# A third transposed tile per state read out by ScalarE and added by GpSimd, in a decoder layer with a selective scan

## The reference

```python
def _selective_scan(u, dt, A, Bm, Cm, D):
    def step(h, xs):
        u_t, dt_t, b_t, c_t = xs
        dA = jnp.exp(dt_t[:, :, None] * A[None])
        h = dA * h + (dt_t * u_t)[:, :, None] * b_t[:, None, :]
        y = jnp.einsum('bds,bs->bd', h, c_t) + D * u_t
        return (h, y)
...
p1 = jnp.einsum('bsh,eoh->bseo', nf, mlp1_weight) + mlp1_bias
g = jnp.minimum(p1[..., 0::2], LIMIT)
lin = jnp.clip(p1[..., 1::2], -LIMIT, LIMIT)
act = g * jax.nn.sigmoid(ALPHA * g) * (lin + 1.0)
p2 = jnp.einsum('bsei,ehi->bseh', act, mlp2_weight) + mlp2_bias
combined = jnp.einsum('bseh,bse->bsh', p2, combine)
```

## Time and profile before

| | us |
|---|---|
| median of 3 runs (lowest, highest) | 1700.97 (1700.62, 1701.95) |
| the profiled execution | 1699.97 |
| its span in the trace | 1698.2 |

### The profile page before, as it was taken

How to read it: one execution, slowest core, us unless ns; L and a number is a source line. 1 busy time by engine, 2 the same in 40 slices (tenths; PEclk the granted TensorE clock), 3 DMA queues, 4 the chain that set the end, 5 groups by cost and what they waited for, 6 DMA issues and landing times.

```text
span 1698.2 us, 23130 instructions
## 1 busy us (share of the span) xinstructions
PE 1314.0 (77%) x5582; PEld 857.7 (51%) x5582; DVE 1405.5 (83%) x1829; ACT 934.7 (55%) x1369; POOL 970.2 (57%) x529
## 2 busy tenths in 40 slices
PE   6965545699877777799867777799867787798698
PEld 4434334466345555566345554566344455466375
DVE  6159999887789999888689999978689999962597
ACT  3264443323777767523777767623777767711464
POOL 1059888630588888620588888621488978620000
PEclk9986666699899989999989889999989979996699
DMA  6111111011111112020111112020211121010111
GB/s 219 54 35 38 37 49 38 28 35 34 63 38 56 56 51 68 7 75 33 52 51 56 47 58 69 7 76 20 65 50 54 39 66 53 25 50 1 63 53 59
DMA packets 53348, 86.13 MB, mean 51 GB/s; under 512 B 8245, under 2 KB 33986, under 8 KB 53259
## 3 DMA queue, kind: packets, MB, share of 16 engines
q1 hardware_dynamic: 49993, 82.89, 15.0%
q10 hardware_dynamic: 3266, 2.21, 0.4%
HBM read 74.51 MB, written 10.57 MB: 50 GB/s over the span
## 4 chain that ended last, share of the span: by engine, by line
PE 38%; DVE 28%; issue 14%; ACT 13%; POOL 4%; DMA 2%; DVEq 1%; ACTq 1%; SPq 0%; POOLq 0%
DVE work L1255 13%; PE ps L1462 12%; PE ps L1656 7%; DVE xt L1255 7%; DVE stage L1293 6%; ACT ps L891 6%; PE ps L1678 4%; PE ps L1628 2%; PE ps L1457 2%; POOL work L642 2%; PE ps L1560 2%; ACT work L922 2%; ACT ps L917 2%; PE ps L1562 2%; PE ps L1470 2%
## 5 line engine op out<-in xcount | busy, mean ns | idle before, releaser
L1656 PE MATMUL ps<-ident,work 128*128 128x128 f32 x1536 | 313.0, 329 | 287.0 <-DVE stage L1293 184.7
L1255 DVE TENSOR_TENSOR_SCAN work<-ps,work 128x1024 f32<-128x1024 f32 x192 | 438.4, 2284 | 19.6 <-ACT ps L891 12.1
L1656 PEld LDWEIGHTS ps<-ident,work 128*128 128x128 f32 x1536 | 191.9, 161 | 418.9 <-DVE stage L1293 246.2
L891 ACT ACTIVATE ps<-dt,a_neg 128x1024 f32<-128x1024 f32 x256 | 284.9, 1117 | 190.9 <-DVE work L1255 149.8
L642 POOL TENSOR_TENSOR work<-dtu,b_bc 128x1024 f32<-128x1024 f32 x128 | 299.9, 2372 | 56.9 <-PE ps L1656 53.1
L1293 DVE SCALAR_TENSOR_TENSOR stage<-ps,c_tok,stage 128x512 f32<-128x512 f32 x384 | 272.4, 734 | 25.6 <-PE ps L1656 23.4
L1678 PE MATMUL ps<-w,work 128*128 (+1 forms) x1024 | 274.8, 418 | 1.8 <-DVE work L1400 1.8
L1678 PEld LDWEIGHTS ps<-w,work 128*128 128x128 f32 x1024 | 219.5, 217 | 52.9 <-issue 9.5
L1628 PE MATMUL ps<-nfT,w 128*128 128x512 bf16 x512 | 169.3, 430 | 32.0 <-DVE work L1330 17.9
L642 POOL TENSOR_TENSOR work<-dtu,w_out 128x1024 f32<-128x1024 f32 x64 | 149.3, 2353 | 44.1 <-PE ps L1656 44.1
L658 POOL TENSOR_TENSOR stage<-stage,work 128x512 f32<-128x512 f32 x128 | 160.2, 1275 | 15.9 <-ACT work L907 15.9
(11 more groups left out here) (142 smaller groups left out, 1937.6 us busy)
## 6 DMA issues: line engine op xcount, KB each, us to landing
b_bc<-b_rows SPq DMA_DIRECT2D x32, 512.0 KB, 3.7
w_out<-b_rows SPq DMA_DIRECT2D x32, 512.0 KB, 4.0
wbc<-combine_rows SPq DMA_DIRECT2D x64, 256.0 KB, 3.4
stage<-in_x SPq DMA_DIRECT2D x8, 512.0 KB, 4.2
xt<-in_x SPq DMA_DIRECT2D x8, 512.0 KB, 5.4
x_rows<-xt SPq DMA_DIRECT2D x4, 1024.0 KB, 4.7
res<-x_rows SPq DMA_DIRECT2D x8, 512.0 KB, 4.1
out_x<-res SPq DMA_DIRECT2D x8, 512.0 KB, 3.3
```

The lines of the kernel that those rows point to most:

```text
L891: act.activation(decay_in(d, alone, opening), dt[:, d, :], ACT.Exp, scale=a_neg[:, bass.ds(it * 2 + (d * N + hf * (N // 2) + par), 1)]).th ...
L1255: dve.tensor_tensor_scan(h, decays, h, 0.0, ALU.mult, ALU.add).then_inc(scan_done, 1)
L1656: mm = pe.transpose(ps[:, a % HT_BANKS, d * P:(d + 1) * P], slot(par, d)[:, a * P:(a + 1) * P], ident[:, :])
```

## The change

Tile 7 (`LATE`) joins tiles 0 and 1 (`EARLY`) in being read out by ScalarE and added by GpSimd; there are three such tiles in a state and still two buffers, used in rotation. VectorE sums tiles 2 to 6. On each engine:
- ACT: evict of tile 7 stands after tanh 1 and add 1, ahead of linear_in 1.
- POOL: the add of tile 7 of a state stands one turn later, after product 0 of that turn; at the end of a row it stands behind the others.
- DVE: sums 2, 3; (scan 1) gate product 0, sum 4; (scan 2) sum 5, linear product 0; (scan 3) sum 6, gate product 1.
- PE: up(1,0) goes ahead of the transposes of tiles 6 and 7; down j=0 follows these. The waits for banks 0 and 1 follow the new readers: tile 1 waits for the evict of tile 7 of the state before, tile 7 for sum 5.

```diff
@@ -189,8 +189,10 @@
         GATE_BANK, LINEAR_BANK = 4, 5
-        EVICTED = 2
+        EARLY, LATE = (0, 1), (TT - 1,)
+        EVICTED = len(EARLY) + len(LATE)
         SUMMED = TT - EVICTED
+        EVICT_BUFFERS = 2
@@ -402,7 +404,8 @@
         ITS = N // 4
-        DBU_CREDIT, SCAN_CREDIT, HT_CREDIT, HT_READY_CREDIT = 8, 4, HT_BANKS, 16
+        DBU_CREDIT, SCAN_CREDIT, HT_CREDIT, HT_READY_CREDIT = 8, 4, 1, 16
+        EVICT_CREDIT = 1
         EX_CREDIT = 2
@@ -573,7 +576,7 @@
             pool.sem_inc(aw_ready, EX_CREDIT)
-            pool.sem_inc(evict_added, EVICTED)
+            pool.sem_inc(evict_added, EVICT_BUFFERS)
             for i, value in enumerate((-LIMIT, ALPHA / 2 * LIMIT, 2 * LIMIT)):
@@ -651,11 +654,12 @@
-                def add_evicted(hf, it, par):
-
-                    for e in range(EVICTED):
-                        pool.wait_ge(evict_ready, (state(b, hf, it, par) - 1) * EVICTED + e + 1)
-                        pool.tensor_tensor(stage[:, e, :], stage[:, e, :], evicted[:, e, :],
+                def add_evicted(hf, it, par, back, tiles):
+
+                    for a in tiles:
+                        e = (EARLY + LATE).index(a)
+                        pool.wait_ge(evict_ready, (state(b, hf, it, par) - back) * EVICTED + (e + 1 + EVICT_CREDIT))
+                        pool.tensor_tensor(stage[:, a, :], stage[:, a, :], evicted[:, (par + back + e) % 2, :],
                                            ALU.add).then_inc(evict_added, 1)
@@ -665,9 +669,12 @@
                     pool.wait_ge(b_loaded[par], (b * 2 * ITS + hf * ITS + it) * 16 + 16)
+                    second = hf == 0 and isinstance(it, int) and it == 0
                     for d in range(CT):
                         state_product(w, par, d)
-                    add_evicted(hf, it, par)
+                        if d == 0 and not second:
+                            add_evicted(hf, it, par, 2, LATE)
+                    add_evicted(hf, it, par, 1, EARLY)
                     if bp is not None:
@@ -676,9 +683,10 @@
                 turns(pool, body)
+                add_evicted(1, ITS, 0, 2, LATE)
                 if bp is not None:
                     weigh(1, ITS, 0)
-                add_evicted(1, ITS, 0)
+                add_evicted(1, ITS, 0, 1, EARLY + LATE)
@@ -687,6 +695,7 @@
             act.sem_inc(l_ready, 1)
+            act.sem_inc(evict_ready, EVICT_CREDIT)
             for dst, name in ((qwT, "qWT"), (cwT, "cWT"), (kwT, "kWT"), (vwT, "vWT"), (owT, "oWT")):
@@ -897,15 +906,16 @@
                     act.wait_ge(dve_scaled, 5)
-                def evict(hf, it, par):
+                def evict(hf, it, par, tiles):
...
                     n = it * 2 + (hf * (N // 2) + par - 1)
-                    wait_apart(act, evict_added, w * EVICTED + EVICTED)
-                    for e in range(EVICTED):
-                        wait_apart(act, hT_ready, w * TT + (e + 1 + HT_READY_CREDIT))
-                        act.activation(evicted[:, e, :], ps[:, e % HT_BANKS, :], ACT.Copy,
-                                       scale=c_tok[:, e, bass.ds(n, 1)]).then_inc(evict_ready, 1)
+                    for a in tiles:
+                        e = (EARLY + LATE).index(a)
+                        wait_apart(act, evict_added, w * EVICTED + (e + 1))
+                        wait_apart(act, hT_ready, w * TT + (a + 1 + HT_READY_CREDIT))
+                        act.activation(evicted[:, (par + 1 + e) % 2, :], ps[:, a % HT_BANKS, :], ACT.Copy,
+                                       scale=c_tok[:, a, bass.ds(n, 1)]).then_inc(evict_ready, 1)
@@ -957,7 +967,7 @@
                         decay(b, bp is None, hf, it, par, 0)
-                    evict(hf, it, par)
+                    evict(hf, it, par, EARLY)
                     if bp is not None:
@@ -972,6 +982,8 @@
                         chains[1][1]()
+                    evict(hf, it, par, LATE)
+                    if bp is not None:
                         linear_in(hf, it, par, 1)
@@ -1002,9 +1014,10 @@
                 turns(act, body)
-                evict(1, ITS, 0)
+                evict(1, ITS, 0, EARLY)
                 if bp is not None:
                     clip(state(bp, 1, ITS, 0) * 2)
+                evict(1, ITS, 0, LATE)
@@ -1354,20 +1367,20 @@
                     scan(w, par, 1, decay_in(1, bp is None))
-                    accumulate(hf, it, par, 4)
-                    accumulate(hf, it, par, 5)
                     if bp is not None:
                         gate_product(s, 0)
+                    accumulate(hf, it, par, 4)
+                    if bp is not None:
                         if second:
...
                     scan(w, par, 2, decay_in(2, bp is None))
-                    accumulate(hf, it, par, 6)
+                    accumulate(hf, it, par, 5)
                     if bp is not None:
...
                     scan(w, par, 3, decay_in(3, bp is None))
-                    accumulate(hf, it, par, 7)
+                    accumulate(hf, it, par, 6)
                     if bp is not None:
@@ -1409,7 +1422,7 @@
                         linear_product(state(bp, 1, ITS, 0) - 1, 1, 1)
-                    for a in range(EVICTED, TT):
+                    for a in range(len(EARLY), TT - len(LATE)):
                         accumulate(1, ITS, 0, a)
@@ -1484,14 +1497,17 @@
-                    pe.wait_ge(hT_used, r * (N * SUMMED) + (N * SUMMED - HT_BANKS + d + 1 + HT_CREDIT))
+                    if d == 0:
+                        pe.wait_ge(hT_used, r * (N * SUMMED) + (N * SUMMED + HT_CREDIT))
+                    else:
+                        pe.wait_ge(evict_ready, r * (N * EVICTED) + (N * EVICTED + EVICT_CREDIT))
                 product(ph.bank(job), [(w_in[:, k, DI + d * P:DI + (d + 1) * P], xnT[:, k, c * HALF:(c + 1) * HALF])
...
-                    pe.wait_ge(evict_added, r * (N * EVICTED) + (N * EVICTED + EVICTED))
+                    pe.wait_ge(evict_added, r * (N * EVICTED) + (N * EVICTED + EVICT_BUFFERS))
                 if job == ("Y", 2, 0):
@@ -1648,10 +1664,12 @@
-                        if EVICTED <= a < 2 * EVICTED:
-                            pe.wait_ge(evict_ready, w * EVICTED + (a - EVICTED + 1))
+                        if a == 0:
+                            pe.wait_ge(hT_used, w * SUMMED + HT_CREDIT)
+                        elif a <= 1 + len(EARLY):
+                            pe.wait_ge(evict_ready, w * EVICTED + (a - 1 + EVICT_CREDIT))
                         else:
-                            pe.wait_ge(hT_used, w * SUMMED + (a + 1 if a < EVICTED else a - EVICTED + 1))
+                            pe.wait_ge(hT_used, w * SUMMED + (a - 1 - len(EARLY) + HT_CREDIT))
                         for d in range(CT):
@@ -1724,11 +1742,11 @@
                         up(hf, it, par, 0, 1)
+                        up(hf, it, par, 1, 0)
                     else:
...
                     if bp is not None:
-                        up(hf, it, par, 1, 0)
                         if hf == 1 and isinstance(it, int) and par == 1:
```

## The result

| | before | after |
|---|---|---|
| median of 4 runs each, us | 1701.46 | 1785.70 |
| lowest and highest | 1700.62, 1702.99 | 1783.95, 1789.98 |
| the profiled execution | 1699.97 | 1789.98 |
| its span | 1698.2 | 1788.2 |

The ratio is 1.0498, with a 95% interval of 1.0476 to 1.0520: the changed kernel is 5% slower, by 84.2 us between the medians. The forecast was 1794 in a range of 1702 to 1832.

What follows compares the result with a forecast made beforehand. VectorE, nearly full in joint turns of 15.66 us, and the decays bounded the kernel. Against the profiled 1699.97, +86 joint turns and row tails, +7 finalize, +7 openings, -6 loop alone gave +94, so 1794, range 1702 to 1832.

Steps and rivals of the forecast that it cites:

- VectorE and the decays: Joint turn: by these alone it falls from 15.66 to 15.30 us, so at most 0.36 is gained.
- The chain: Joint turn: from sum 5 over tile 7, down 0, up(1,1), linear_in 1 to decay 0; turn 15.69 full clock, 18.4 low.
- the share of low clock: Joint turn: low clock for four fifths of the chain, so 2.2 us more, a turn of 17.8.
- The clock: TensorE before tile 7: 1.25 us busy in 5.9 brings the clock down; rival that it stays up, 1704 us, chance 0.10.
- The three finalize turns: Joint turns with finalize: tile 7 moves behind one scan, 2.4 us each, 7 in all.
- The turns that open a joint loop: First turn with transposes in each joint row: same chain, 2.5 us each, 7 in all.
- The row ends: Tail of each joint row: counted as one more joint turn, 2.2 us each.
- The loop alone: Loop without joint phases: turns fall from 13.57 to about 13.1 us, -6 in all, between 0 and -9.
- this ring: Loop alone: scan 3, transposes, evict, transposes; VectorE waits 0.60 us for tile 2; claimed not to be shortened.
- GpSimd and ScalarE: Joint turn: GpSimd's added 1.25 us makes 15.4, under 15.66; ScalarE's added evict of 0.68 costs nothing by itself.
- ordinary turns: Joint turns: 36, or 39 with the row tails, each 2.2 us longer; 86 us for the 39.
- the cases: Whole time: forecast 0.76, clock stays up 0.10, faster 0.08 plus 0.02 for a mistake, slower still 0.06.

Runs made afterwards that it cites:

- the filled kernel: The changed kernel with up(0,1) computed and tile 6 transposed four times over in joint turns; 1708.39 us, ratio 1.0049.
- the filled kernel with linear_in 1 moved: The filled kernel with linear_in 1 of a turn run behind decay 0 of the next; 1708.68 us, ratio 1.0039.
- the filled run with tile 7 early: The changed kernel with sums 4 and 5 ahead of scan 2, PE reordered, up(0,1) computed four times over in joint turns; 1704.79 us, ratio 1.0022.

## Why the prediction was right

**VectorE and the decays.** The step from 15.66 to 15.30 by these alone fits the gaps that were measured: in the changed kernel the four scans start 4.11, 3.72 and 3.74 apart (542.32, 546.43, 550.15, 553.89), and it is the last gap that grew, to 5.59. No run reached 15.30 in every turn, since others ended later; the nearest were the short turns of 15.35 in the filled kernel with linear_in 1 moved.

**The chain.** The start of tile 7 was put at 10.82 after scan 0 and came at 10.82. The full-clock end was put at 15.69 and measured at 15.67 in the filled kernel. With the clock as granted I said 17.8, and the turns are 16.9 to 17.7, with 18.4 behind the finalize turn. The mean of the 36 is 17.3, 1.6 over before instead of 2.2. The term was mis-sized in the share of low clock: I took four fifths of the chain, 2.2 of 2.7. In the turn shown, 17.16 long, 1.5 of the 2.7 came. Tile 7 took the whole of its low-clock price (0.91 to down 0); down 0 took 2.73, between 1.73 and the 3.57; up(1,1) and what follows ran at the full clock.

**The clock.** The forecast rested on the earlier trace rows: a stretch in which PE had little work, without any idle time over some 2.2, and then the low clock. In the changed kernel the two idle times are 2.17 and 1.84 (I had put them at 2.1 and 2.5), hardly longer than the 2.15 of the earlier trace rows. Yet the clock fell in every ordinary turn: the granted clock of each in the first joint row is 0.80 or 0.81, where before it was 0.89 in eight turns of the twelve and 1.00 in four. The filled kernel settles it: same chain, same waits, PE busier by its repeats, and 77 of the 84 us are gone. The repeats also shorten the idle times, from 2.17 to 0.88 and from 1.84 to 1.17, so the run shows that PE's thin stretch brings the clock down, not whether its work or its gaps do. By the Trainium skill, "TensorE: Matmul & The Clock Gate", "What's actually happening", activity releases the throttle; the filled kernel agrees, with PEclk from 0.78 to 0.96. The reading of its section "HAM oscillation — how this bites in real kernels" by single long idle gaps does not hold here, where the clock falls with no gap over 2.17 in an ordinary turn, and the measurement decides.

**The other turns.** The three finalize turns cost 4.3 each (25.1 against 20.8), not 2.4; the late add had a share of 1.7 in this by its own run, which I had counted at nothing there. The turns that open a joint loop cost 7.9 in all, I had said 7 (2.5 x 3 is 7.5). The row ends cost 9.9, I had said 2.2 each.

**The loop alone.** I said -6 and it was -0.7. The step that failed is the start of the next scan 0 at 13.0 to 13.1 behind product 0: turns are 13.3 to 13.7. Two terms failed. From the end of sum 5 to product 0 I took 0.9 for tile 7, and it is about 1.3, with a granted clock of 0.50 in that stretch. And tile 0 now waits for sum 6, which stands behind scan 3, where it had waited for a sum ahead of it: the change moved the last reader of bank 0 behind the last scan. From scan 3 to sum 2 it is now 6.29 (285.69 to 291.98) where it was 5.71 (176.62 to 182.33), which takes back nearly all of the 0.65 that VectorE lost. I had said only that this ring was not shortened; that part of it was made longer. The run with sum 6 small shows that neither of the two sets the turn alone.

**GpSimd and ScalarE.** Right in ordinary turns: they have room in a turn of 17, as the run with the small add shows. Where tile 7 was early again they did not: GpSimd waits for its evict in the run with sum 5 put back, and ScalarE holds the turn of 15.64 in the filled run with tile 7 early. The prediction had no term for the late add's own wait for its evict.

**The sum.** Forecast +94 against the profiled execution, measured +90.0: ordinary turns 79 against 57.6 (58.6 in the 36, less 1.0 by which the last turns, up to the end of scan 3, got shorter), row ends 7 against 9.9, finalize 7 against 12.9, openings 7 against 7.9, loop alone -6 against -0.7, and 2.4 at the start and behind the loop alone that no term had. Between the medians it is +84.2. The total is nearer than its terms deserve, which is luck: 21 too much in the ordinary turns stand against 10 too little in the row ends, finalize turns and openings, 5 in the loop alone and 2 elsewhere. Two small slips in the working changed nothing: the chances of the cases add up to 1.02, and by them slower would be 0.87, not 0.84; and 1745 belongs to a turn of 16.6, not 16.8, once the other terms are added.

## What to carry to other kernels

When an instruction moves, ask who stands in fixed order behind the one that it releases: taking 0.65 us of VectorE's work out of each turn cost 1.6, because one sum stood behind one scan more and the chain behind it met the low clock. Where a trace shows the clock low behind stretches with little work on PE, a chain that moves there is to be priced at the low clock. The longest idle time didn't foretell it here: it was 2.15 before and 2.17 after. Redundant matmuls in idle time are a cheap test of this: here the time fell by 77 us when work was added, so the clock was the price.

## What I had not expected of the hardware

The fall came with the turn: in the stretch shown, 6.8 to 6.9 us at 0.5 and 10.2 at 1.0, repeating every 17.1, in step with turns of 17.0 to 17.3. Turns also stayed at 17.0 to 17.1 when the link over linear_in 1 was cut and when the late add was made small. Whether the two hold each other in step isn't shown by any run.

Adding 18 matmuls to each joint turn of the changed kernel (6 for up(0,1), 12 for tile 6), some 2.7 us of PE time, took 1.5 us off the turn. In the kernel before, the 6 for up(0,1) changed nothing (1.0004).
